# Summing the first half of a quantised weight on four engines: TensorE takes 21 of 31 levels, fed by VectorE masks and ScalarE diagonals

## The reference, cut to what matters

```python
# cond: O = I = 2048, GROUP = 128, 32 entries in the codebook
lora_delta = lora_B @ lora_A * (32.0 / 64)
cb = codebook / max(|codebook|, 1e-8)
scale = exp(scale_log)                           # one for each row and group of 128
wg = (weight + lora_delta) grouped by 128
normalized = wg / scale
thresholds = (cb[:-1] + cb[1:]) * 0.5            # 31
quantized = cb[searchsorted(thresholds, normalized, side='left')]
w_eff = quantized * scale + lora_delta
y = x @ w_eff.T
# ffn: y @ W_base.T + b, and a routed low-rank term of 8 experts and rank 16
```

## Time and profile before

| | |
|---|---|
| median of three runs | 2389.96 us |
| profiled execution | 2390.88 us |
| its span | 2389.1 us |
| PE busy | 2318.9 us (97%) |
| DVE busy | 1708.0 us (71%) |
| ACT busy | 1427.1 us (60%) |
| POOL busy | 1270.6 us (53%) |

### The profile page before, as it was taken

One profiled execution on the slowest core, in us unless ns is written; L12 is line 12 of the kernel. 1 busy time (PEld: TensorE's weight loads), 2 busy tenths in 40 slices (PEclk: granted clock), 3 DMA queues, 4 the chain that ended last, 5 costly groups with the idle time before them and its releaser, 6 DMA issues.

```text
span 2389.1 us, 30759 instructions
## 1 busy us (share of the span) xinstructions
PE 2318.9 (97%) x11678; PEld 2102.9 (88%) x11678; DVE 1708.0 (71%) x2021; ACT 1427.1 (60%) x1799; POOL 1270.6 (53%) x704
## 2 busy tenths in 40 slices
PE   3989899999999999999999999999999999999999
PEld 2445479999999999999999999999999989999998
DVE  8899998999978868777868967878873333333333
ACT  7999978989977656665646657566643321111111
POOL 6989847779874437777764436777760000111010
PEclk9989999999999999999999999999999999999999
DMA  5788854443343435766764436667664334545554
GB/s 198 272 274 277 309 208 162 162 166 141 138 149 114 118 116 197 238 230 225 234 219 123 119 105 200 222 232 238 221 208 128 102 96 161 197 180 198 185 195 152
DMA packets 121561, 442.58 MB, mean 185 GB/s; under 512 B 12818, under 2 KB 53330, under 8 KB 84562
## 3 DMA queue, kind: packets, MB, share of 16 engines
q1 hardware_dynamic: 121412, 440.61, 54.4%
HBM read 289.43 MB, written 151.13 MB: 184 GB/s over the span
## 4 chain that ended last, share of the span: by engine, by line
PE 91%; DVE 4%; ACT 3%; POOL 1%; issue 0%; DMA 0%; SPq 0%; DVEq 0%; POOLq 0%; ACTq 0%
PE m L777 20%; PE m L776 20%; PE m L778 20%; PE m L761 8%; PE m L762 8%; PE m L760 8%; PE m L703 4%; DVE acc L1115 3%; ACT mk L918 2%; PE m L806 1%; ACT mp L924 1%; PE pd L682 0%; DMA lb<-in_lb 0%; PE pd L683 0%; ACT ds L906 0%
## 5 line engine op out<-in xcount | busy, mean ns | idle before, releaser
L1115 DVE SCALAR_TENSOR_TENSOR acc<-mk,dj,acc 128x1024 f32<-128x1024 uint8 x736 | 944.9, 1284 | 91.6 <-ACT mk L918 72.1
L776 PE MATMUL m<-gh,xh 128*128 128x384 f32 (+2 forms) x2560 | 903.2, 353 | 0.0
L777 PE MATMUL m<-gl,xh 128*128 128x384 f32 (+2 forms) x2560 | 898.7, 351 | 0.0
L778 PE MATMUL m<-gh,xl 128*128 128x384 f32 (+2 forms) x2560 | 896.0, 350 | 0.0
L918 ACT ACTIVATE mk<-wr,bj 128x1024 uint8<-128x1024 f32 x768 | 843.8, 1139 | 0.7 <-DVE acc L1115 0.7
L776 PEld LDWEIGHTS m<-gh,xh 128*128 128x128 f32 x2560 | 481.6, 188 | 23.5
L778 PEld LDWEIGHTS m<-gh,xl 128*128 128x128 f32 x2560 | 480.9, 188 | 23.6
L777 PEld LDWEIGHTS m<-gl,xh 128*128 128x128 f32 x2560 | 481.4, 188 | 21.2
L1315 POOL TENSOR_TENSOR pp<-pp,tm 128x1024 f32<-128x1024 f32 x192 | 466.4, 2429 | 22.0
L1335 POOL TENSOR_TENSOR xl<-xw,xh 128x512 fp32r<-128x512 f32 x96 | 124.1, 1294 | 564.7 <-ACT xh L972 564.4
L1302 POOL TENSOR_SCALAR tm<-mp,dj 128x1024 f32<-128x1024 uint8 x224 | 258.1, 1152 | 246.5 <-ACT mp L924 235.6
(11 more groups left out here) (131 smaller groups left out, 1781.3 us busy)
## 6 DMA issues: line engine op xcount, KB each, us to landing
part<-part SPq DMA_DIRECT2D x192, 1036.0 KB, 6.7
rows<-in_wb SPq DMA_DIRECT2D x61, 1036.0 KB, 4.8
xw<-in_x SPq DMA_DIRECT2D x128, 256.0 KB, 3.2
out<-part SPq DMA_DIRECT2D x31, 1024.0 KB, 4.2
kw<-in_wb SPq DMA_DIRECT2D x138, 192.0 KB, 2.4
wr<-in_w SPq DMA_DIRECT2D x32, 512.0 KB, 8.8
dl<-delta SPq DMA_DIRECT2D x30, 512.0 KB, 5.9
delta<-ds SPq DMA_DIRECT2D x24, 512.0 KB, 3.2
```

Of the source, the lines that this page charges most:

```text
L776: e.matmul(R.m[c][:, 0:w], xh, gh, start=k == 0, stop=False)
L777: e.matmul(R.m[c][:, 0:w], xh, gl, start=False, stop=False)
L778: done = e.matmul(R.m[c][:, 0:w], xl, gh, start=False, stop=stop and k == n - 1)
L1115: e.scalar_tensor_tensor(R.acc, R.mk[k % NM], R.dj[:, j:j + 1], R.acc, ALU.mult, ALU.add).then_inc(S["ac"], 1)
```

## The change

Only the first half (`q` = 0) is summed differently. All other halves keep 24 levels on VectorE and 7 on GpSimd.

- Of its 31 levels, TensorE takes `NV0` = 21, VectorE five (`SUM_AT`), GpSimd `NP0` = 5.
- A TensorE level: VectorE compares the half with the threshold, times 255, into a float32r mask `mq` of 128x1024 in a ring of `NMQ` = 4. ScalarE scales the identity by the step into two 128x128 diagonals, for the high and the low part of the step (`dg`), five levels ahead. TensorE multiplies: two diagonals by two column halves of 512, four matmuls a level, accumulated in two PSUM banks `sums`.
- GpSimd splits the steps into high and low parts (`djh`, `djl`) before its first own work.
- VectorE adds `sums` to `pp` and then `acc`, `cb[0]` and `pp` into `wr`.
- All copies of the wide deltas go to ScalarE; VectorE's `lora_a(0)` moves behind mask 1, and the reciprocal of 128x240 scales behind mask 3.

```diff
+NP0 = 5
+SUM_AT, SUM_MASK_AT = (2, 6, 10, 14, 18), (0, 2, 4, 6, 8)
+NV0 = NJ - NP0 - len(SUM_AT)
+NMQ, DIAG_AHEAD = 4, 5
-FIRST_AT, EARLY_AT = (1, 3, 5, 8, 11, 14, 17), (0, 1, 3, 6, 10, 13, 16)
+FIRST_AT, EARLY_AT = (0, 1, 3, 5, 9), (0, 1, 3, 6, 10, 13, 16)
...
-        for j in range(NV):
+        for j in range(NV if q else NV0):
...
-    late = [(0, j) for j in range(6, 22, 2)] + ...
+    late = [(0, j) for j in range(3, 18, 2)] + ...
 def on_vector(n):
-    return n < 4
+    return n < 0
```

TensorE:

```diff
+    def level(j):
+        e.wait_ge(S["mq"], j + 1)
+        e.wait_ge(S["dg"], 2 * j + 2)
+        for k in range(2):
+            for h in range(2):
+                at = slice(512 * h, 512 * h + 512)
+                done = e.matmul(R.sums[:, at], R.dg[j][k], R.mq[j % NMQ][:, at], start=j == 0 and k == 0,
+                                stop=j == NV0 - 1 and k == 1)
+        done.then_inc(S["pl"], 1)
...
         if what == "unit":
+            if at[0] == 0:
+                level(at[1])
             if at in DELTA_AT:
                 wide(DELTA_AT[at])
```

ScalarE (for later halves `unit` is as before):

```diff
+    def diagonal(j):
+        if j == 0:
+            e.wait_ge(S["id"], 16)
+            e.wait_ge(S["djl"], 1)
+        e.activation(R.dg[j][0], R.idn, ACT.Copy, scale=R.dj[:, j:j + 1]).then_inc(S["dg"], 1)
+        e.activation(R.dg[j][1], R.idn, ACT.Copy, scale=R.djl[:, j:j + 1]).then_inc(S["dg"], 1)
...
+        if q == 0 and j + DIAG_AHEAD < NV0:
+            diagonal(j + DIAG_AHEAD)
...
+        if q == 0 and j in SUM_MASK_AT:
+            k = SUM_MASK_AT.index(j)
+            col = NV0 + k
+            e.activation(R.mk[k], w, ACT.Identity, bias=R.bj[:, col:col + 1], scale=GROW).then_inc(S["mk"], 1)
...
     narrow(0)
     narrow(1)
+    for j in range(DIAG_AHEAD):
+        diagonal(j)
     lora_b(0)
     lora_a(0)
     narrow(2)
...
-            if at == (0, 10):
+            if at == (0, 4):
                 lora_b(1)
```

VectorE:

```diff
-    next(scales)
-    lora_a(0)
...
+    def first_mask(j):
+        if j == 0:
+            e.wait_ge(S["n"], 1)
+            e.wait_ge(S["bk"], BOOK_READY - 1)
+        if j >= NMQ:
+            e.wait_ge(S["pl"], j - NMQ + 1)
+        e.tensor_scalar(R.mq[j % NMQ], R.wr[0], R.u[:, j + 1:j + 2], FULL, ALU.is_gt, ALU.mult).then_inc(S["mq"], 1)
+        if j in SUM_AT:
+            k = SUM_AT.index(j)
+            step = R.dj[:, NV0 + k:NV0 + k + 1]
+            e.wait_ge(S["mk"], k + 1)
+            if k == 0:
+                e.scalar_tensor_tensor(R.acc, R.mk[k], step, R.wr[0], ALU.mult, ALU.subtract).then_inc(S["ac"], 1)
+            else:
+                e.wait_ge(S["ac"], k)
+                e.scalar_tensor_tensor(R.acc, R.mk[k], step, R.acc, ALU.mult, ALU.add).then_inc(S["ac"], 1)
+        if j == NV0 - 1:
+            e.wait_ge(S["ac"], len(SUM_AT))
+            e.wait_ge(S["pp"], NP0)
+            e.wait_ge(S["pl"], NV0)
+            e.tensor_tensor(R.pp, R.sums, R.pp, ALU.add).then_inc(S["fq"], 1)
+            e.wait_ge(S["fq"], 1)
+            e.scalar_tensor_tensor(R.wr[0], R.acc, R.cn[:, 0:1], R.pp, ALU.add, ALU.add).then_inc(S["cl"], 1)
...
-            unit(*at)
+            if at[0]:
+                unit(*at)
+            else:
+                first_mask(at[1])
+            if at == (0, 1):
+                lora_a(0)
+            if at == (0, NMQ - 1):
+                next(scales)
```

GpSimd (its levels of the first half are at `SPARE_AT[:5]`, that is units 0, 3, 6, 10 and 13):

```diff
-    e.wait_ge(S["ac"], 1)
+    e.wait_ge(S["bk"], 10)
+    e.tensor_copy(R.djh, R.dj).then_inc(S["djh"], 1)
+    e.wait_ge(S["djh"], 1)
+    e.tensor_tensor(R.djl, R.dj, R.djh.bitcast(F32), ALU.subtract).then_inc(S["djl"], 1)
+    e.wait_ge(S["mq"], 1)
     lora_b(0)
...
-            if at == (0, 11):
+            if at == (0, 7):
                 lora_b(1)
```

More of the change, by code:

```diff
@@ L215, in __init__ @@
         self.gl = [self.take(f"gl{k}", DX, F32R) for k in range(NMAX)]
+        at_gh, at_gl = self.top - 8 * NMAX * DX, self.top - 4 * NMAX * DX
+        self.dg = [[self.put(f"dg{j}_{k}", at_gh + 1024 * j + 512 * k, 128, F32R) for k in range(2)] for j in range(NV0)]
+        assert 1024 * NV0 <= 4 * DX * (NMAX - 1) + 4096
+        self.mq = [self.put(f"mq{k}", at_gl + 4096 * k, H, F32R) for k in range(NMQ)]
         at_x = [self.space(NMAX * 512) for _ in range(3)]
@@ L254, in __init__ @@
         self.sm = self.take("sm", 2)
+        self.djh = self.take("djh", NJ, F32R)
+        self.djl = self.take("djl", NJ)
         assert self.top <= nc.sbuf_usable_end
@@ L272, in __init__ @@
         self.pd = bank("pd")
-        self.m = [bank(f"m{c}") for c in range(NCH)]
+        banks = bank("m", NCH)
+        self.m = [banks[:, c * 512:(c + 1) * 512] for c in range(NCH)]
+        self.sums = banks[:, 0:H]
         self.pz, self.pm, self.p5 = self.acc[:, 0:512], self.acc[:, 512:1024], self.pd
@@ L346, in delta_places @@
 def delta_places():
-    late = [(0, j) for j in range(6, 22, 2)] + [(1, j) for j in range(1, 7)] + [(2, 3), (2, 4)]
+    late = [(0, j) for j in range(3, 18, 2)] + [(1, j) for j in range(1, 7)] + [(2, 3), (2, 4)]
     late += [(q, j) for q in range(3, 2 * N0) for j in range(3, 7)]
@@ L364, in on_vector, with level_of, pool_level, pool_count @@
 def on_vector(n):
-    return n < 4
+    return n < 0
 def unit_at(n):
     return n + NARROW
+def level_of(q, j):
+    return len(SUM_AT) + NV * (q - 1) + j if q else j
+def pool_level(q, i):
+    return NP0 * (q > 0) + NP * max(q - 1, 0) + i
+def pool_count(q):
+    return NP if q else NP0
+def pool_column(q, i):
+    return NJ - pool_count(q) + i
 def mask_places(q):
@@ L379, in scaled_level @@
 def scaled_level(q, i):
-    return (NP * q + i) % 2 if q < 2 * N0 else 0
+    return pool_level(q, i) % 2 if q < 2 * N0 else 0
 def raw_of(q):
@@ L908, in wide @@
                      scale=0.5).then_inc(S["dl"], 1)
+    def diagonal(j):
[4 more added lines that the diff above has]
+        e.activation(R.dg[j][1], R.idn, ACT.Copy, scale=R.djl[:, j:j + 1]).then_inc(S["dg"], 1)
     def unit(q, j):
-        k, w = NV * q + j, R.wr[raw_of(q)]
+        k, w = level_of(q, j), R.wr[raw_of(q)]
         if j == 0:
@@ L915, in unit @@
                 e.wait_ge(S["bk"], BOOK_READY)
-        if k >= NM:
-            e.wait_ge(S["ac"], k - NM + 1)
-        e.activation(R.mk[k % NM], w, ACT.Identity, bias=R.bj[:, j:j + 1], scale=GROW).then_inc(S["mk"], 1)
+        if q == 0 and j + DIAG_AHEAD < NV0:
+            diagonal(j + DIAG_AHEAD)
+        if q:
+            if k >= NM:
+                e.wait_ge(S["ac"], k - NM + 1)
+            e.activation(R.mk[k % NM], w, ACT.Identity, bias=R.bj[:, j:j + 1], scale=GROW).then_inc(S["mk"], 1)
         if j in mask_places(q):
             i = mask_places(q).index(j)
-            k = NP * q + i
+            k, col = pool_level(q, i), pool_column(q, i)
             if k >= 2:
                 e.wait_ge(S["tm"], k - 1)
-            e.activation(R.mp[k % 2], w, ACT.Identity, bias=R.bj[:, NV + i:NV + i + 1], scale=GROW).then_inc(S["mp"], 1)
+            e.activation(R.mp[k % 2], w, ACT.Identity, bias=R.bj[:, col:col + 1], scale=GROW).then_inc(S["mp"], 1)
+        if q == 0 and j in SUM_MASK_AT:
+            k = SUM_MASK_AT.index(j)
+            col = NV0 + k
+            e.activation(R.mk[k], w, ACT.Identity, bias=R.bj[:, col:col + 1], scale=GROW).then_inc(S["mk"], 1)
     def split(q):
@@ L983, in low_weights @@
         e.wait_ge(S["cl"], NQ)
-        e.wait_ge(S["pp"], NP * NQ)
+        e.wait_ge(S["pp"], pool_level(NQ, 0))
         e.activation(R.bs, R.bw[0:96, :], ACT.Copy).then_inc(S["bshi"], 1)
@@ L1100, in wide @@
                         R.pd[:, 0:128 * many].rearrange("p (b i) -> p b i", b=many), 0.5, None, ALU.mult).then_inc(S["dl"], 1)
+    def first_mask(j):
[21 more added lines that the diff above has]
+            e.scalar_tensor_tensor(R.wr[0], R.acc, R.cn[:, 0:1], R.pp, ALU.add, ALU.add).then_inc(S["cl"], 1)
     def unit(q, j):
-        k = NV * q + j
-        if q >= 2 * N0 or k == 0:
+        k = level_of(q, j)
+        if q >= 2 * N0 or (q, j) == (1, 0):
             e.wait_ge(S["mk"], k + 1)
@@ L1120, in unit @@
                 e.wait_ge(S["mk"], k + 2)
-            e.wait_ge(S["pp"], NP * (q + 1))
+            e.wait_ge(S["pp"], pool_level(q + 1, 0))
             e.scalar_tensor_tensor(R.wr[raw_of(q)], R.acc, R.cn[:, 0:1], R.pp, ALU.add, ALU.add).then_inc(S["cl"], 1)
@@ L1301, in spare_scaled @@
             e.wait_ge(S["pp"], k - 1)
-        e.tensor_scalar(R.tm[scaled_level(q, i)], R.mp[k % 2], R.dj[:, NV + i:NV + i + 1], 0.0, ALU.mult, ALU.add).then_inc(S["tm"], 1)
+        e.tensor_scalar(R.tm[scaled_level(q, i)], R.mp[k % 2], R.dj[:, col:col + 1], 0.0, ALU.mult, ALU.add).then_inc(S["tm"], 1)
     def spare_added(q, i):
-        k = NP * q + i
+        k = pool_level(q, i)
         if i == 0:
@@ L1319, in effective @@
         if q < 2 * N0:
-            e.wait_ge(S["ac"], NV * (q + 1) + 1)
+            e.wait_ge(S["ac"], level_of(q + 1, 0) + 1)
         else:
@@ L1358, in gpsimd_program @@
             q, j = at
-            if j in SPARE_AT:
```

(3 more changed lines are left out.)

## The result

The changed kernel takes 2399.17 us (median of five runs, 2398.01 to 2399.90) against 2389.96 us before: a ratio of 1.0037, with a 95% interval of 1.0022 to 1.0052. It is slower by 9.2 us, where 8 us were forecast (2398 us); at 0.4% that is small, but the interval lies clear of 1. Its profiled execution took 2399.90 us with a span of 2397.7 us.

A forecast was written before the change was run, and what follows sets the result against it. PE was 91% of the chain; the change moves the first half's end, `cl`. From 19.1 us, 41.5 us on shared ports led to 65.5 us taken, +8.2 us passed on: 2398 us median, range 2395 to 2403, for 8 in 10 2385 to 2403.

The forecast's parts named there:

- The late start: First half's start: diagonals wait for the identity, landing at 15.1 us, so `lbh` starts at 18.1 us instead of 13.3.
- A mask's own price: DVE in the first half: a one-source 128x1024 comparison runs at twice the rate and takes 0.69 us.
- The exclusion: First half: DVE's masks and POOL's instructions contend and go one after the other; chance 0.5.
- The sum: First half from 19.1 us: POOL 26.4, masks 13.1, `las` 0.7, a DVE level 1.3, together 41.5 us; `cl` at 63.1 earliest.
- upper case: First half: only one mask between two POOL instructions, POOL through at about 55 us, some 12 masks made, `cl` at 70 us.
- mostly one by one, with some masks back to back: First half's end: the value taken between the bounds 63.1 and 70 us, `cl` at 65.5 us, +8.2 us.
- TensorE's clock: PE's first-half levels, four matmuls each: 1.71 us at the low clock level or 0.86 us at the high one.
- The rival in which it bounds alone: First half: PE stays at the low clock and bounds by itself, `cl` 64.6 us, 2397 us; chance 0.1.
- One to one: After the first half: a shift of `cl` reaches the kernel's end in full, as the second half has no slack.
- The lead of ACT into the second half: ACT begins the second half before `cl`, 4.7 us in the old kernel; claimed to stay about that, nothing added.
- up to 3 us: Plain-rate rival: ACT ends its first half near 48 us, so up to 3 us come back in the second half.
- masks at the plain rate: First half: masks cost 1.2 us, leave POOL alone and DVE bounds; `cl` 56.5 us, 2388 us; chance 0.2.

The follow-up runs named there:

- half the matmuls: Changed kernel with two matmuls a TensorE level instead of four, low-part diagonals built but not multiplied; 2398.00 us, ratio 1.0029 to the kernel before.
- plain masks: Changed kernel with each mask made from two inputs, the half from SBUF and a constant 255 from PSUM; 2387.75 us, ratio 0.9992 to the kernel before.
- no POOL levels: Changed kernel with POOL's five first-half levels given to TensorE (26 there, five on VectorE); 2387.56 us, ratio 0.9989 to the kernel before.

## Why the prediction was right, point by point

**The late start.** The identity landed at 15.7 us (15.1 forecast), the diagonals came one every 0.29 us (0.30), and `lbh` started at 18.6 us (18.1). Of the size: taking it away brought `cl` 4.9 us earlier, of which 0.6 is that this execution's identity was later than forecast.

**A mask's own price.** 0.69 us forecast from the 128x256 form, 0.75 us measured (minimum 0.74). The double rate was right; the 0.06 us may be the price of the per-partition operand, which the 128x256 form doesn't have, but no run parts that.

**The exclusion.** Forecast from instructions with two SBUF inputs, it holds for the one-source comparison: the masks' maximum is 2.86 us beside a minimum of 0.74, and the run that reads one stream from SBUF has neither the long masks nor the long POOL instructions. The rule of the Trainium skill ("SBUF — State Buffer", section "Who interferes with whom") is that a VectorE instruction in a two-port mode and one of GpSimd block each other, the second for the whole of the first. This trace agrees: nine masks that began inside a POOL instruction ended 0.55 us after it, and none of them before.

**The sum.** POOL was through its levels at 52.2 us; of the 19 masks ten were made and the eleventh ended at 52.7. The forecast's upper case, strictly one mask between two POOL instructions, had about 55 us and 12 masks. From there to `cl` it had 15 us, and 14.6 were measured, with a wait for TensorE of 3.34 us inside it. So what happened is the upper case throughout, and the forecast of 65.5 us, "mostly one by one, with some masks back to back", assumed a mixture that didn't occur: from 27.68 us until POOL was through, every mask waited out a POOL instruction. What made up for it is a term that the upper case had too long. A turn was counted as a whole mask, 0.69 us, but cost POOL's next instruction 0.3 to 0.5 us, and POOL was done 3 us sooner. `cl` at 66.7 us is 1.2 from the 65.5 taken, inside 63.1 to 70; the mechanism was right, but that it came as near as that is luck.

**TensorE's clock.** The forecast left open which of the two levels would hold; both did, in turn. Of the levels that PE started after a wait, those at 38.30 and 50.00 us took 1.96 and 2.07 us, and those at 43.85 and 46.16 us 1.19 and 1.20; in an unbroken row they took 1.7 us at the low level and 0.93 us at the high one. The granted clock (the column before the last two) goes with it:

```profile
42.00:48.60 6.60, 3.48 (x13) 1.91 (x11) 6.60 (x4) 4.76 (x11) 6.52 (x4) 1.00 0.23 74
48.80:55.40 6.60, 5.40 (x12) 3.96 (x13) 6.60 (x6) 1.76 (x5) 3.29 (x2) 0.50 0.13 43
55.60:66.70 11.10, 9.04 (x40) 7.00 (x39) 7.38 (x9) 7.77 (x13) 1.68 (x2) 1.00 0.27 94
```

The rival in which it bounds alone fell with the run of half the matmuls.

**One to one.** `cl` moved by 9.4 us, the eighth half's write by 7.9, the span by 8.6 and the median by 9.2. So halves 2 to 8 gave 1.5 us back, 0.7 came again behind them, and 0.4 lies outside the span, which the forecast took as unchanged: 2.2 us against 1.8. That the median moved almost as `cl` did is the sum of these, not a shift passed on untouched. The lead of ACT into the second half was forecast as unchanged: 4.9 us against 4.7. Its last wide copy waited as foreseen, but ACT as a whole, worked out to end near 46 us, ended at 61.8: it waited 15.3 us for TensorE's wide products, which stand behind masks. Where ACT led by 6.5 us (plain masks, from 48.44) or 7.8 us (no POOL levels, from 47.84), the second half took 35.1 and 35.5 us. So 1.9 to 2.4 of the rival's "up to 3 us" came back, though not in the order of the leads.

**The rival "masks at the plain rate"** was no case of the change, but as an experiment it came at 2387.75 us, where 2388 was worked out. That is partly luck: `cl` was 54.9 us instead of 56.5, and with 2.4 us back in the second half the rival's own way of adding gives some 2385.5.

The same difference stands in every run with masks: against the kernel before, the median gained 0.2 to 2.7 us less (or lost more) than the eighth half's write did in the profiled execution. For the plain masks it is 4.9 us there and 2.5 in the median. The record splits this up. From the end of the eighth half's write to the end of the span it is 2075.8 us before and 2076.5 here. Outside the span there are 1.7 to 1.9 us in all executions of the kernel before and of the kernels without POOL levels, and 2.2 to 2.4 in all of the others. The remaining 1.3 us are how far the two profiled executions lay from their medians, one above and one below. What adds the 0.4 and the 0.7 us stays open.

## What to carry to other kernels

Moving work to an engine with idle time is free only if the instruction that feeds it does not contend with what the others do: look in the trace for the same instruction with a mean far above its minimum. An instruction of half the rate that stays off the shared ports can beat one of the full rate that waits its turn (a mean of 1.27 against 1.54 us here). And a tile that nobody needed early before, like the identity, gets a place in the load order when it becomes the first thing needed.

## What the runs showed of the hardware

A comparison of 128x1024 float32 with a per-partition threshold and a second constant operation, written as float32r, takes 0.75 us when it begins with POOL quiet and up to 2.86 us when it begins while POOL is in a 128x1024 instruction; it then ends 0.55 us after that instruction. Against a POOL queue that is never empty it got one turn for each POOL instruction, not several. The same comparison with a second input from PSUM took 1.18 to 1.28 us, undisturbed.

The load of 64 KB issued at 5.8 us landed between 7.9 and 9.9 us later in the executions that left it there, and 4.3 to 5.9 us after its issue when it was sixth.

On ScalarE, building a 128x128 diagonal with a per-partition scale takes 0.39 us, and one every 0.29 us in a row.
